# Cross attention in three layers: value products split evenly over the tiles, the square turn as two instructions, GpSimd's copies ahead of its rotation, and five transfers issued by ScalarE

## What is computed

```python
q_big  = einsum('bshk,hkq->bshq', (hidden_q @ Wq.T).reshape(b, s, 16, 128), w_kc_q)
kv     = kv_c * cos + rotate_half(kv_c) * sin          # keys and values are the same rows
scores = einsum('bhsr,bhlr->bhsl', einsum('bshq,hqr->bhsr', q_big, W_qr),
                                   einsum('bld,hdr->bhlr', kv, W_kr))
ctx_c  = einsum('bhsl,bld->bhsd', softmax(scores, axis=-1), kv)     # 1500 keys, 64 wide
out    = einsum('bhsd,hkd->bshk', ctx_c, w_kc_kv).reshape(b, s, 2048) @ Wo.T
```

## Time and profile before

| | us |
|---|---|
| median of three runs | 3237.76 |
| the three runs | 3200.05, 3239.22, 3237.76 |
| the execution that was profiled | 3230.32 |
| its span, first to last instruction | 3228.3 |
| its loop of batches 1 to 14: layer 0, layer 1, layer 2 | 390.19, 363.29, 367.39 |
| busy: TensorE, VectorE, ScalarE, GpSimd | 2933.8, 1862.5, 1242.3, 872.7 |

### The profile page before, as it was taken

How to read it: one execution, slowest core, us unless ns; L and a number is a source line. 1 busy time by engine, 2 the same in 40 slices (tenths; PEclk the granted TensorE clock), 3 DMA queues, 4 the chain that set the end, 5 groups by cost and what they waited for, 6 DMA issues and landing times. The chain is left out here.

```text
span 3228.3 us, 47818 instructions
## 1 busy us (share of the span) xinstructions
PE 2933.8 (91%) x17993; PEld 1709.2 (53%) x17997; DVE 1862.5 (58%) x3321; ACT 1242.3 (38%) x1997; POOL 872.7 (27%) x743
## 2 busy tenths in 40 slices
PE   4889998988999989899998989989899998677999
PEld 3655555554455453355555557753355555446444
DVE  6557887733232257788885233347788885655222
ACT  3446656521111142455554122222455653424221
POOL 4324555410316024433333000004333333201000
PEclk8899999988999989999999999999999999888999
DMA  1146677622122212277776010012277775001111
GB/s 32 48 120 161 166 174 166 145 66 95 63 91 78 88 28 81 62 165 158 158 165 162 13 42 25 25 43 74 65 170 155 166 168 125 15 12 23 39 39 33
DMA packets 221440, 299.21 MB, mean 93 GB/s; under 512 B 127178, under 2 KB 149052, under 8 KB 218764
## 3 DMA queue, kind: packets, MB, share of 16 engines
q1 hardware_dynamic: 220348, 294.39, 37.4%
q10 hardware_dynamic: 864, 1.77, 0.2%
HBM read 120.52 MB, written 21.38 MB: 44 GB/s over the span
## 5 line engine op out<-in xcount | busy, mean ns | idle before, releaser
L1786 ACT ACTIVATE l1x_shared<-l1x_shared,l1x_a_low 128x1500 f32<-128x1500 f32 x112 | 173.1, 1546 | 159.8 <-DVE l1x_shared L1740 156.9
L1786 ACT ACTIVATE l2x_shared<-l2x_shared,l2x_a_low 128x1500 f32<-128x1500 f32 x112 | 173.1, 1546 | 158.4 <-DVE l2x_shared L1740 156.8
L1786 ACT ACTIVATE l0x_shared<-l0x_shared,l0x_a_low 128x1500 f32<-128x1500 f32 x112 | 173.2, 1546 | 139.5 <-DVE l0x_shared L1740 138.1
L1656 PE MATMUL l0x_a_S_ps<-l0x_kt,l0x_a_q 64*128 64x366 f32 (+1 forms) x896 | 176.4, 507 | 4.4 <-issue 2.5
L1656 PE MATMUL l1x_a_S_ps<-l1x_kt,l1x_a_q 64*128 64x366 f32 (+1 forms) x896 | 175.9, 506 | 2.2 <-DVE l1x_shared L1740 1.9
L1656 PE MATMUL l2x_a_S_ps<-l2x_kt,l2x_a_q 64*128 64x366 f32 (+1 forms) x896 | 174.9, 505 | 2.0 <-DVE l2x_shared L1740 1.6
L2026 DVE TENSOR_TENSOR l0f_times_up<-l0f_gate,l0f_U 128x448 f32<-128x448 f32 x64 | 39.7, 621 | 236.9 <-PE l0f_U L1944 236.9
L1995 ACT ACTIVATE l0f_gate<-l0f_G 128x448 f32<-128x448 f32 x72 | 39.1, 543 | 310.7 <-PE l0f_G L1939 310.7
L1353 POOL TENSOR_TENSOR l2x_q_straight<-l2x_q_straight,l2x_q_crossed 128x448 f32<-128x448 f32 x48 | 54.5, 1135 | 340.5 <-DVE l2x_q_crossed L1344 340.5
L1740 DVE TENSOR_SCALAR_CACHE_REDUCE l0x_shared<-l0x_a_S_ps 128x768 f32<-128x768 f32 x112 | 107.3, 958 | 66.0 <-PE l0x_a_S_ps L1656 57.4
L1740 DVE TENSOR_SCALAR_CACHE_REDUCE l2x_shared<-l2x_a_S_ps 128x768 f32<-128x768 f32 x112 | 107.3, 958 | 53.7 <-PE l2x_a_S_ps L1656 50.2
(11 more groups left out here) (672 smaller groups left out, 6474.2 us busy)
## 6 DMA issues: line engine op xcount, KB each, us to landing
l0x_space<-normed SPq DMA_DIRECT2D x192, 128.0 KB
l1x_space<-normed SPq DMA_DIRECT2D x192, 128.0 KB
l2x_space<-normed SPq DMA_DIRECT2D x192, 128.0 KB
l0x_space<-l0x_a_blocks SPq DMA_DIRECT2D x186, 96.0 KB, 2.8
l1x_space<-l1x_a_blocks SPq DMA_DIRECT2D x186, 96.0 KB, 3.6
l2x_space<-l2x_a_blocks SPq DMA_DIRECT2D x186, 96.0 KB, 3.3
l0f_gu<-in_L_ffn_gu SPq DMA_DIRECT2D x36, 256.0 KB, 2.6
l0x_a_q<-l0x_qa SPq DMA_DIRECT2D x32, 224.0 KB, 4.0
```

The lines of the kernel that those rows point to most:

```text
L1656: last = pe.matmul(S_ps[:, 2 * pair + rows_, 0:w], q[lane, b % 2, k * 128:(k + 1) * 128], kt[lane, b % 2, pair * W1:pair * W1 + w], start= ...
L1786: act.activation(p[:, n % 2], p[:, n % 2], ACT.Exp, bias=low[:, n % 2, 1:2], scale=-1.0, accum_out=den[:, b % 2, k:k + 1]).then_inc(exp_re ...
```

## The change

Four things are edited in `attend`; the arithmetic, its order within a sum and all sizes of transfers stay as they are.

1. `PIECES` is a new table. Instead of four slots (eight products) after five of the tiles and two slots after tiles 5 and 6, every tile has 3 or 4 slots, so that the columns are nearly equal. The last piece of a batch now stands under tile 5 of the next batch instead of tile 4; `keep_contexts` follows by one tile.
2. `block_turn` is two instructions, squares 1 to 6 of the 8 middle blocks first, then squares 0 and 7, each with a semaphore of its own. The first pair of `negate` waits for the first of them only; the second pair, which writes over the outer squares, waits for the second.
3. GpSimd does `own(b, 0)` before `rope(b + 2)`; the copies of group 0 no longer wait for the rotation.
4. ScalarE issues the store and the fetch of the inverses and the fetch of the queries, after tiles 1 and 5. They are gone from SyncE's list.

```diff
-    PIECES = {5: (0, 0, 2), 6: (0, 2, 4), 7: (0, 4, 8), 8: (0, 8, 12), 9: (1, 0, 4), 10: (1, 4, 8), 11: (1, 8, 12)}
+    PIECES = {5: [(0, 0, 1)], 6: [(0, 1, 4)], 7: [(0, 4, 7)], 8: [(0, 7, 10)], 9: [(0, 10, 12), (1, 0, 1)],
+              10: [(1, 1, 5)], 11: [(1, 5, 9)], 12: [(1, 9, 12)]}
...
@@ SyncE
                 for b in range(B):
                     move(sp, b, 0, range(4))
-                    if b > 0:
-                        fetch_inverses(b - 1)
-                    if b + 2 < B:
+                    if ctx is None and b + 2 < B:
                         sp.wait_ge(scored, 2 * (T * b + 6) + 2)
-                        fetch_queries(b + 2)
-                        if ctx is None:
-                            ahead.fetch_keys(sp, b + 2)
+                        ahead.fetch_keys(sp, b + 2)
...
                     move(sp, b, 1, range(4) if b + 1 < B else range(2))
-                    if b + 1 < B:
-                        store_inverses(b)
@@ GpSimd
-                        pool.wait_ge(kept_own, 8 * (b - 2))
+                    pool.wait_ge(kept_own, 8 * (b - 2) + 4)
...
-                        pool.wait_ge(roped, min(b + 3, B))
+                        pool.wait_ge(roped, min(b + 2 + g, B))
...
                 for b in range(B):
+                    own(b, 0)
                     if ctx is not None and b + 2 < B:
                         rope(b + 2)
-                    own(b, 0)
                     if b > 0:
                         scatter(b - 1)
                     own(b, 1)
@@ TensorE
-                    if k > 4:
-                        values(b, *PIECES[k])
-                    elif b > 0:
-                        values(b - 1, *PIECES[k + T])
+                    for piece in PIECES.get(k + T, []) if b > 0 else []:
+                        values(b - 1, *piece)
+                    for piece in PIECES.get(k, []):
+                        values(b, *piece)
@@ VectorE
                         if pair == 0 and n > 1:
                             dve.wait_ge(turned, n - 1)
-                            dve.wait_ge(blocked, n - 1)
+                            dve.wait_ge(inner_blocked, n - 1)
                         if pair == 1:
                             dve.wait_ge(passed, 2 * n + 1)
+                            if n > 1:
+                                dve.wait_ge(outer_blocked, n - 1)
...
-                    dve.transpose(blocks[g][:, :, k - FIRST[g]].rearrange("q l j b -> q j l b"),
-                                  p[:, n % 2, 2 * KP:LK - 2 * KP].rearrange("q (j l b) -> q j l b", j=NB, l=4)).then_inc(blocked, 1)
+                    to = blocks[g][:, :, k - FIRST[g]].rearrange("q l j b -> q j l b")
+                    squares = p[:, n % 2, 2 * KP:LK - 2 * KP].rearrange("q (j l b) -> q j l b", j=NB, l=4)
+                    dve.transpose(to[:, 1:NB - 1], squares[:, 1:NB - 1]).then_inc(inner_blocked, 1)
+                    dve.transpose(to[:, 0:NB:NB - 1], squares[:, 0:NB:NB - 1]).then_inc(outer_blocked, 1)
@@ ScalarE
-                    if k == 2 and b > 0:
+                    if k == 3 and b > 0:
                         keep_contexts(b - 1, 0)
-                    if k == 5 and b > 0:
+                    if k == 6 and b > 0:
                         keep_contexts(b - 1, 1)
...
                         exp(n + 2)
+                    if k == 1 and b > 0:
+                        store_inverses(b - 1)
+                    if k == 5 and b > 0:
+                        fetch_inverses(b - 1)
+                    if k == 5 and b + 2 < B:
+                        act.wait_ge(scored, 2 * (T * b + 6) + 2)
+                        fetch_queries(act, b + 2)
```

54 lines of the change are left out of this document (29 added, 25 removed).

## The result

The changed kernel takes 3293.43 us (median of 4 runs, 3275.44 to 3298.43) against 3234.0 us of the kernel before beside it on the same chip (4 runs, 3200.05 to 3239.22). The ratio is 1.020, 95% interval 1.015 to 1.026: slower. Whether by more than the 2% that was called the bound of what can be told, the interval leaves open. The profiled execution has a span of 3292.7 us, 64.4 more than before.

What follows compares the result with a forecast made beforehand. The prediction took TensorE as the bound, losing time in waits, mainly for moved squares. Layers 1 and 2 -33, split turn -2, layer 0 +9 (-9 + 18), ScalarE +3 gave -23 us: 3230.32 to 3207 us, range 3172 to 3255.

Steps and rivals of the forecast that it cites:

- ScalarE's issues, +3 us: ScalarE's added DMA issues after tiles 1 and 5: covered with 0.1 us to spare; bounds 0 and 17 us, 3 taken.
- transfers in ScalarE's queue that delay the moves beside them: Closing caveat on ScalarE's queue: would make the sum wrong in a way no profile row prices; no size given.
- Layer 0, +18 us for a late landing: Layer 0, group 1's moves behind the delayed rotation: new wait of 0.4 to 2.1 us in 14 batches, 1.3 taken.
- Land 2.8 us after issue: Layer 0, group 1's moves: assumed landing time, putting the squares at t5 (start of tile 5's turn) + 21.3 to 23.0.
- Rival C: Layer 0: moves land late by 3.5 us, lower clock costs another 1, 63 us in all; 3252 us, chance 0.10.
- SyncE's queue, layers 1 and 2, -33 us: SyncE without inverses and queries starts group 1's moves 2.1 us earlier, winning 33 of 37.7 us of TensorE's lost time.
- Rival B: Layers 1 and 2: lateness lies in the transfers, not queue order; only 9 us won there, 3231 us, chance 0.18.
- the later need: Layers 1 and 2: new pieces need group 1's squares 0.95 us later, nine waits, 9 us if only this helps.
- Even pieces, 0: TensorE's value products: evened tiles of 3.43 to 3.65 us, batch again 24.8 us, no gain without waits.
- GpSimd's order, -9 us: Layer 0: copying first removes VectorE's wait for GpSimd, 3 us taken, plus 6 of 7.5 us of waits for squares.
- Split turn, -2 us: VectorE's square turn in two: nothing in the loops, -0.15 to +0.02 us on each of 18 first-batch tiles.
- Rival D: ScalarE late in every batch: TensorE loses 1.5 us at tile 8, 63 us instead of 3; 3267 us, chance 0.05.

Runs made afterwards that it cites:

- e1: Changed kernel with the store of the inverses back on SyncE, behind the moves of group 1: 3224.91 us, ratio 0.995.
- e9: Changed kernel with the inverses turned by VectorE and stored as 28 pieces of 128 bytes, same queue and place: 3162.24 us, ratio 0.985.
- e3: Kernel before with only the store of the inverses given to ScalarE after tile 1: 3302.05 us, one run.
- e6: Changed kernel with the store of the inverses on SyncE behind the moves, turned by VectorE into 28 pieces of 128 bytes: 3168.81 us, ratio 0.977.
- e7: Kernel before with only the new table of value pieces and the context copies one tile later: 3283.60 us, one run.
- e5: Kernel before with the inverses turned by VectorE and stored by SyncE as 28 pieces of 128 bytes: 3174.91 us, ratio 0.980.
- e4: Kernel before with the inverses stored as 128 rows of 28 bytes, read back in the old order: 3185.18 us, one run.

## Why the prediction was wrong

I predicted 3207 us, a range of 3172 to 3255, and a chance of 0.03 for a loss of over 2%. The time is 3293.43. The sum was -23 us where +59 were measured.

- **The step that failed.** "After tile 1 one DMA", in the term "ScalarE's issues, +3 us": I priced the store of the inverses as 0.75 us of issue and looked neither at what it writes nor at its landing, which the trace of before had at 8.4 us in its list of issues. The code said it too, with a transposed destination marked as slow and non-contiguous. The prediction's last part named "transfers in ScalarE's queue that delay the moves beside them" as a way to be wrong and gave it no chance. e1 (store back: -84.9 us in layer 0) and e9 (store in another form, nothing else: -92.7) show that this is the loss; e3 shows that it needs nothing else of the change.
- **Layer 0, +18 us for a late landing.** The chain was right in each of its times up to the last issue: t5 + 10.35 to 18.1. With the last issue at t5 + 18.1, a landing 2.8 us later is t5 + 20.9, just in time for t5 + 20.95. "Land 2.8 us after issue" was wrong in the changed kernel (6.9) and right without the element store (e6: 3.04 or less, no wait). So the term is 0 by itself and was 81.5 with the store. Rival C had the place, the slot 4 of group 1 in every batch, and the clock at its lower level behind it (0.50 here, 0.52 in the earlier trace rows); its mechanism, the late start, isn't there.
- **SyncE's queue, layers 1 and 2, -33 us.** Nothing came. The moves do start earlier, as forecast: in the median of layer 1 at t5 + 4.94, where I had said 4.85, and before at t5 + 7.33. But the twelve take 9.1 us in the median of the loop, against 8.1 before, so that they are through 1.4 us earlier and not 2.4. It goes with ScalarE's four issues beside them: in the runs that have these in layers 1 and 2 the medians are 8.8 to 9.5 us, in those that have not 7.6 to 8.3. More to the point, waits that end with a store's landing are not shortened by earlier moves; 11 were left where 9 had been. Rival B, "what made some batches late is in the transfers themselves", was the right doubt, with 0.18. Its price of 9 us for the later need was wrong as well: the store moved along. I had read the nine waits as lateness of the moves, though in the same rows twelve moves were issued by 1424.71 and TensorE still waited at 1432.44: 7.7 us, where the median landing was 2.8 to 3.6. That comparison was open to me.
- **Even pieces, 0.** Right for batches without a wait, 24.76 us. e7 shows a price that the sum didn't hold apart: without GpSimd's new order the table costs 69 us in layer 0.
- **GpSimd's order, -9 us.** VectorE's wait for the copies is gone, as expected; the waits for squares that I booked as won became 56.8 us.
- **Split turn, -2 us.** Right in kind: 0.21 us a tile where VectorE sets the time, a little more than the 0.15 I gave as the bound, since the negation also overlaps the second turn. The second instruction adds 0.13 us of busy time, where I had 0.17; at my own 1 ns an element gives 1.24 - 1.02 = 0.22, so that reading was loose as well. The first batches are shorter by 3.2, 0.7 and 1.0 us; of the 3.2 some 2.5 were a wait at its tile 5 that before's profile had and e5's has not.
- **ScalarE's issues, +3 us.** 0 for the issues themselves. No tile 8 waits for ScalarE: in the rows above its queue issues the inverses for 1.31 us while the exponential of 1.54 runs. The two of the queries, 1.16 us from 505.66 on, run beside nothing, and ScalarE stands idle for 1.33 us; that much it could spare. Rival D falls with it.

The Trainium skill, "DMA: Bandwidth & Descriptors", section "Queues, rings and completion order", has the rule that I should have weighed: the increment of a transfer's semaphore is a strongly ordered write that lands only after every earlier write of that DMA engine, across its queues. By it a move on SyncE's queue isn't complete before the element writes of ScalarE's queue that went ahead of it on the same DMA engine. In the changed kernel's layer 0 and in e3, where the store goes out on the other queue among or near the moves, the runs agree (waits of up to 5.3 and 7.3 us), and without the single elements the waits are gone (e4, e9). The rule as it stands does not cover the kernel before and e1: there the store is issued behind the last move on the same queue, and 24 waits still ended 4.4 to 10.0 us after its issue. The rule quoted in the prediction, that queues of several engines share the same DMA engines, is borne out too; I drew too small a price from it.

**Open.** The increments come late when the packets are through; whether the bytes of the squares were in place by then is not shown, since no run reads them without waiting for the count. Why a store that is issued behind the last move holds its completion is not shown either. Why the store takes 8 to 9 us, with packets that fill 4.3% of the engines' time, is not shown. Nor is it why some batches of layers 1 and 2 escape, every other one in e3, and why e1's layer 2 loses 12 us more than before's, with 7 such waits where there were 5.

## What to carry to other kernels

Price a transfer by its landing and by its number of separate pieces, not by its bytes or its issue: a 3.5 KB store of single elements took 8 to 9 us and made others late that carry the critical data. Where a wait ends long after the awaited transfer's issue (6 to 10 us in most of the waits here, where landings take about 3), look at what else is in flight, and move or reshape that. A small vector can be turned on VectorE for 0.21 us, so that its store has whole rows; do that before choosing a queue for it.

## What was not expected of the hardware

- 896 elements of 4 bytes landed 8.4 to 9.0 us after issue, the same 3.5 KB in 128 rows of 28 bytes in 1.8 to 2.3 us (medians of the layers).
- Completions came up to 8.2 us after the last packet of the moves (0.3 us in the median of batches without a wait), with the DMA engines idle for 3.2 us of it in one batch.
- While a store of 4.3% busy time was under way, the DMA engines moved 60 GB/s at a busy share of 0.82 (137 GB/s at 0.65 over that loop).
- ScalarE's queue issued two DMAs (1.31 us), in e9 also four (1.64 us), beside a running exponential of 1.54 us, without lengthening it.
- Two turns of 768 and 256 elements (0.97 and 0.40 us) made a tile of VectorE 0.21 us shorter than one of 1024 (1.24 us).
- Twelve moves took SyncE 9.1 us to issue in layer 1 while ScalarE's queue issued beside it, 8.1 without (medians).
